# A graph-attention edge loop: q expanded by three bf16 products, item tables from DRAM

## The chip, the cores and the metric

One core of a Trainium2 chip runs the kernel, with its engines TensorE (PE), VectorE (DVE), ScalarE (ACT), GpSimd (POOL) and SyncE (SP), which work side by side and meet at semaphores. The metric is the device time of one execution in microseconds (us); lower is better. The time of a kernel is the median of its runs.

## The reference

Two layers on 6,250 nodes of 256 numbers, with 106,250 edges that are sorted by their destination node `dst`. First an attention over the edges, with 8 heads of 32, then a small mixture of 8 experts. What the change touches is the first:

```python
xn = layernorm(x)
q, k, v = xn @ Wq + bq, xn @ Wk + bk, xn @ Wv + bv       # per node, split in 8 heads of 32
e = edge_attr @ We                                       # per edge
alpha = sum(q[dst] * (k[src] + e), per head) / sqrt(32)  # per edge and head
alpha = softmax of alpha over the edges of one dst
out[dst] += (v[src] + e) * alpha                         # per node
x = x + out + xn @ Ws + bs
x = x + top-2-of-8 experts of layernorm(x)
```

## The kernel before

**Stages.** The program runs in stages, each a block with its own semaphores, one after the other. (1) The edge lists are cut into work items. (2) The projection: for each of 49 tiles of 128 nodes, q stays in SBUF as float32 (`q_sb`), k and v go to DRAM as `vk_table`, and the skip term goes to `skip_table`. (3) The edge loop. (4) Gates, layernorm and routing. (5) The experts, 105 blocks. (6) The output. The buffers of small tables in the later stages lie over those of the first: `src_idx`, `dst_loc`, `mask` and `q_sb` are used again under other names.

**Items.** An item is 128 edges and one tile of 128 nodes. A tile of 128 edges that spans two node tiles makes two items. There are 880 items in 55 chunks of 16. The loop is unrolled in the program over chunks (`c`) and items (`i`), and `par` is the chunk's parity.

**What an item does, in the order of its data:**
- SP loads 128 rows of `edge_attr` (`a_ring`, four deep, L727). POOL gathers 128 rows of v and k from `vk_table` by the indices `idx_c` (`kv_ring`, four deep, L743).
- PE turns `a_ring` by two transposes (L875), and ACT copies them to SBUF (`aT`, L827).
- PE multiplies `aT` by `We` into the left half of `ps_e` (two float32 products, L887). It then expands q: the one-hot `selT` (node by edge) times the node tile's q gives each edge the q of its destination, in the right half of `ps_e` (one float32 product of 256 columns, L890, with a column offset `n` in a register). The one-hot is made by ACT for four items at a time (`SEL = 4`), as relu(1 - |row - loc|), by L790 and L799, from `loc_c`, which SP loads for a whole chunk (bf16 numbers, broadcast to all partitions, L698).
- DVE adds e to v and k (`ve_ke`, L967), multiplies k by q (`kqq`, L973), and one item later reduces by head into `alpha` (L956).
- A chunk later, when the softmax of the chunk is known: POOL weighs v by the exponentials (`w_ring`, L753), ACT makes the one-hot of the other direction (`sel`, L805 and L809), PE sums by node (`ps_u`, L936), and DVE adds into `acc` (L1033).

**The softmax of a chunk** is spread over items of the next one by the tables `parts` of each engine. PE makes keys at item 0, scores at 3, minima at 6 and `turn_scores` at 10. DVE scans forward at 3 and back at 4, does `own` at 6, `least` at 7 and `shift` at 8. ACT makes `apart` at 3, `offs` at 4 and the exponentials at 11. POOL applies the mask at 5. DVE does these after the kqq of the same item, and the add to `acc` comes last.

**What sets the order.** Every engine runs its own list in order. PE's list for item i is: turn item i + 1, project item i (L887, L890), a softmax part if there is one, the sum of an item 13 behind. Its project of item i waits for ACT's `aT` of i and for DVE's `ve_added` and `kq_ready` of item i - 2, since `ps_e` has two buffers. The gather of item i waits for `ve_added` of item i - 4. These waits can be read in:

```python
pe.wait_ge(s["aT_ready"], at("aT_ready", c * CH + i))
pe.wait_ge(s["ve_added"], at("ve_added", c * CH + (i - 2)))
pe.wait_ge(s["kq_ready"], at("kq_ready", c * CH + (i - 2)))
```

PE runs a float32 product as two passes, so L887 shows four records an item and L890 two; a transpose shows one. In the projection, PE makes four products of 512 columns a tile (eight passes, L527), ACT copies the turned tile (L503), DVE adds the biases and stores k and v, skip and q (L561 to L565), and SP stores to DRAM.

Of the kernel before, what the change touches and what calls it, by code (L numbers as in the profile page):

```python
# [12 lines left out]
P = 128  # L13
# [16 lines left out]
def gnn_ffn(nc, x, src, dst, edge_attr, Wq, bq, Wk, bk, Wv, bv, We, Ws, bs, Wg, bg, gbias, W1, b1, W2, b2, out):  # L30
# [22 lines left out]
    with ExitStack() as ctx:  # L53
# [56 lines left out]
        loc_table = dram("loc_table", (NCH, CH * P), BF16)  # L110
# [9 lines left out]
        src_idx = sb("src_idx", [P, IT], I32)  # L120
        dst_loc = sb("dst_loc", [P, IT])
        mask = sb("mask", [P, IT])
        item_node_tile = sb("item_node_tile", [1, IT], I32)
        item_row = sb("item_row", [1, IT], I32)
        chunk_tile = sb("chunk_tile", [P, NCH])

        assert NT * NE <= IT and TOP * NT <= IT and NB <= IT
        assert 2 * NB <= IT
        take_i = src_idx[:, 0:NB]
        put_i = src_idx[:, NB:2 * NB]  # L130
        gate_w = dst_loc[:, 0:TOP * NT].rearrange("p (k j) -> p k j", k=TOP)
        logits = mask[:, 0:NT * NE].rearrange("p (j e) -> p j e", e=NE)
        block_expert = item_row[0:1, 0:NB]
        q_sb = sb("q_sb", [P, NT + 1, D])
# [12 lines left out]
        b4 = sb("b4", [P, 4 * D], F32, c_w4)  # L147
        tail_zeroed = sem("tail_zeroed", c_w4)
# [8 lines left out]
        with ExitStack() as c1:  # L157
# [29 lines left out]
            src_g = sb1("src_g", [P, IB, P], I32)  # L187
            sel_g = sb1("sel_g", [P, IB, P], I32)
            run_g = sb1("run_g", [P, IB, P], I32)
# [3 lines left out]
            m_lo = sb1("m_lo", [P, IT])  # L193
            m_hi = sb1("m_hi", [P, IT])
            run_h = flat(q_sb[:, :, :])[:, 0:IB * H * P].rearrange("p (b h e) -> p b h e", h=H, e=P)
            rest = flat(q_sb[:, :, :])[:, IB * H * P:]
# [47 lines left out]
            def _(sp):  # L244
# [16 lines left out]
                with nc.allow_non_contiguous_dma(reason="the short tail row of the edge lists"):  # L261
# [50 lines left out]
            def _(dve):  # L312
# [55 lines left out]
                v.tensor_copy(item_node_tile[:, :], node_tile_rep[0:1, :])  # L368
# [3 lines left out]
                v.tensor_copy(item_row[:, :], r_rep[0:1, :])  # L372
# [13 lines left out]
                for b in range(IB):  # L386
                    n = rows_in(b)
                    dve.wait_ge(turned, b + 1)
                    v.tensor_copy(src_idx[:, b * P:b * P + n], ps_src[:, 0:n])
                    v.tensor_copy(first_run[:, b * P // CH:(b * P + n) // CH], ps_src[:, P:P + n:CH])  # L390
                    v.tensor_copy(last_run[:, b * P // CH:(b * P + n) // CH], ps_src[:, 2 * P + CH - 1:2 * P + n:CH])
                    v.scalar_tensor_tensor(out=dst_loc[:, b * P:b * P + n], in0=node_tile_rep[:, b * P:b * P + n],
                                           scalar=-float(P), in1=ps_sel[:, 0:n], op0=ALU.mult,
# [4 lines left out]
                v.tensor_scalar(m_lo[:, :], dst_loc[:, :], 0.0, BIG, ALU.is_lt, ALU.mult)  # L398
                then(v.tensor_scalar(m_hi[:, :], dst_loc[:, :], P - 0.5, BIG, ALU.is_gt, ALU.mult))
                then(v.tensor_tensor(mask[:, :], m_lo[:, :], m_hi[:, :], ALU.add))  # L400
# [46 lines left out]
        with ExitStack() as c2:  # L447
# [3 lines left out]
            def ps2(name, shape):  # L451
# [14 lines left out]
            skip_out = [sb2(f"skip_out{i}", [P, D]) for i in range(2)]  # L466
            ps_t = [ps2(f"ps_t{i}", [P, 512]) for i in range(2)]
            ps_p = [ps2(f"ps_p{i}", [P, 1024]) for i in range(2)]
            s, at, grant = counters(c2, stat_ready=0, aggregated=0, ln_step=0, var_ready=0, sd_ready=0, xn_ready=0, xn_turned=2,
                                    xnT_ready=2, projected=2, q_out=2, kv_out_ready=2, skip_half=2, skip_out_ready=0,  # L470
# [12 lines left out]
            def _(sp):  # L483
# [8 lines left out]
                sp.wait_ge(stored[1], 16 + 32 * (NT // 2))  # L492

            @block.scalar
            def _(act):
# [1187 lines left out]
```

## Time and profile before

| | |
|---|---|
| median of 3 runs | 2812.76 us (2811.62 to 2814.19) |
| profiled execution | 2812.57 us, its span 2810.8 us |
| PE busy | 2503.2 us, 89% of the span |
| DVE busy | 2038.0 us, 73% |
| POOL busy | 1720.7 us, 61% |
| ACT busy | 1542.6 us, 55% |
| HBM | 173 GB/s over the span |
| mean granted PE clock | 0.952 of full |

Busy time is the time in which an engine executes. Registers, branches, semaphores and the issue of DMAs are not counted. The ends of matmuls are modelled, so records of PE overlap, and it is the distance between starts that tells the pace. An engine's idle time costs something only when that engine, or one that waits for it, is the bottleneck.

### The profile page before, as it was taken

Reading aid. Unit: us, or ns where it says so; the run is one execution under the profiler, and the core shown is the slowest. Engines: PE = TensorE matmul, PEld = TensorE weight load, DVE = VectorE, ACT = ScalarE, POOL = GpSimd, SP = SyncE. Lnnn points to the kernel's source line nnn. Section 1 sums busy time; section 2 is a strip of 40 time slices with the busy share of each in tenths; the row PEclk is TensorE's granted clock in tenths of the full one; section 3 lists DMA queues with packets and bytes.
Section 4 is the critical chain, followed back from the end, with each engine's and each line's share of the span. In section 5 each row is a group of like instructions: output and inputs, shape, how many; then the busy total and the mean of one; then the engine's idle time right before and its main releaser. Section 6 shows DMA issues by size and latency. Waiting matters only on the chain. (4 is left out here: it accounts for less than half of the span.)

```text
span 2810.8 us, 66316 instructions
## 1 busy us (share of the span) xinstructions
PE 2503.2 (89%) x13236; PEld 2104.1 (75%) x13237; DVE 2038.0 (73%) x5145; ACT 1542.6 (55%) x4238; POOL 1720.7 (61%) x2078
## 2 busy tenths in 40 slices
PE   1599699999999999999999999999994848999980
PEld 0244488888888888888888888888882837999980
DVE  2655689899999999999999999998996781111116
ACT  1011266666666666666666666666663224666650
POOL 3000278778788888888888888878886013555540
PEclk9999899999999999999999999999997568999995
DMA  6032577777777777777777777777771612222218
GB/s 215 33 109 107 161 226 212 210 212 215 216 215 213 212 213 212 217 214 218 215 208 216 211 214 221 214 211 209 213 206 58 206 58 66 71 71 69 71 60 274
DMA packets 304072, 490.05 MB, mean 174 GB/s; under 512 B 52058, under 2 KB 217692, under 8 KB 303580
## 3 DMA queue, kind: packets, MB, share of 16 engines
q0 software_dynamic: 81152, 259.63, 32.7%
q1 hardware_dynamic: 215548, 214.12, 23.6%
q10 hardware_dynamic: 7056, 12.85, 1.5%
q8 instruction: 105, 1.72, 0.3%
q14 instruction: 211, 1.73, 0.2%
HBM read 435.86 MB, written 51.41 MB: 173 GB/s over the span
## 5 line engine op out<-in xcount | busy, mean ns | idle before, releaser
L743 POOL DMA_INDIRECT kv_ring<-vk_table,idx_c x880 | 873.6, 993 | 601.3 <-DMA idx_c<-src_idx 238.6
L887 PE MATMUL ps_e<-we_sb,aT 128*128 128x256 f32 x3520 | 910.8, 381 | 12.5 <-DVE kqq L973 11.1
L967 DVE TENSOR_TENSOR ve_ke<-kv_ring,ps_e 128x512 f32<-128x512 f32 x880 | 601.8, 684 | 137.2 <-PE ps_e L890 116.8
L887 PEld LDWEIGHTS ps_e<-we_sb,aT 128*128 128x128 f32 x3520 | 602.2, 191 | 62.1 <-issue 12.7
L753 POOL TENSOR_TENSOR w_ring<-ve_ke,ea 128x264 f32<-128x264 f32 x880 | 558.8, 638 | 22.6 <-PE ps_u L936 6.2
L827 ACT COPY aT<-ps_t 128x256 f32<-128x256 f32 x880 | 326.5, 371 | 433.1 <-PE ps_t L875 422.4
L936 PE MATMUL ps_u<-w_ring,sel 128*128 128x264 f32 x1760 | 539.3, 388 | 8.1 <-DVE acc L1033 5.4
L890 PE MATMUL ps_e<-q_sb,selT 128*128 x1760 | 525.2, 380 | 0.0
L1033 DVE TENSOR_TENSOR acc<-acc,ps_u 128x264 f32 x880 | 369.2, 420 | 23.9 <-DVE acc L1021 12.1
L956 DVE TENSOR_REDUCE alpha<-kqq 128x8 f32<-128x256 f32 x880 | 366.4, 416 | 6.3 <-issue 4.2
L890 PEld LDWEIGHTS ps_e<-q_sb,selT 128*128 128x128 f32 x1760 | 335.6, 191 | 46.0
L973 DVE TENSOR_TENSOR kqq<-ve_ke,ps_e 128x256 f32<-128x256 f32 x880 | 361.2, 410 | 1.9
L936 PEld LDWEIGHTS ps_u<-w_ring,sel 128*128 128x128 f32 x1760 | 316.9, 191 | 57.5 <-POOL w_ring L753 16.4
L805 ACT ACTIVATE apart<-iota_free,dst_loc 128x128 f32<-128x128 f32 x880 | 348.8, 396 | 4.4 <-PE ps_u L936 4.1
L875 PE MATMUL ps_t<-ident,a_ring 128*128 128x128 f32 x1760 | 337.2, 274 | 13.4 <-DMA a_ring<-in_edge_attr 13.4
L875 PEld LDWEIGHTS ps_t<-ident,a_ring 128*128 128x128 f32 x1760 | 248.5, 142 | 115.2 <-DMA a_ring<-in_edge_attr 15.2
L809 ACT ACTIVATE sel<-apart 128x128 f32<-128x128 f32 x880 | 272.5, 310 | 105.6 <-ACT apart L805 2.8
L1611 DVE TENSOR_TENSOR y<-ps_y,acc 128x256 f32<-128x256 f32 x105 | 44.6, 425 | 361.2 <-PE ps_y L1580 361.2
L1494 POOL DMA_INDIRECT t_in<-xn_table,src_idx x105 | 102.5, 976 | 193.7 <-PE ps_t L1563 155.5
L1572 PE MATMUL ps_h<-tT,acc 128*128 128x128 f32 x1680 | 207.5, 277 | 1.8 <-ACT tT L1522 1.8
L1572 PEld LDWEIGHTS ps_h<-tT,acc 128*128 128x128 f32 x1680 | 198.6, 194 | 2.2 <-ACT tT L1522 2.2
L1580 PE MATMUL ps_y<-w_sb,hT 128*128 x840 | 198.6, 379 | 0.0
(248 smaller groups left out, 2538.1 us busy)
## 6 DMA issues: line engine op xcount, KB each, us to landing
a_ring<-in_edge_attr SPq DMA_DIRECT2D x880, 128.0 KB
loc_c<-loc_table SPq DMA_DIRECT2D x55, 512.0 KB, 5.9
kv_ring<-vk_table,idx_c POOLq DMA_INDIRECT x880
vk_table<-kv_out SPq DMA_DIRECT2D x49, 256.0 KB, 2.0
got<-y_table ACTq DMA_DIRECT2D x49, 256.0 KB, 3.8
skip_table<-skip_out SPq DMA_DIRECT2D x49, 128.0 KB, 1.7
skip<-skip_table SPq DMA_DIRECT2D x7, 896.0 KB, 7.2
xn_table<-acc SPq DMA_DIRECT2D x7, 896.0 KB, 4.9
```

Of the source, the lines that this page charges most:

```text
L743: g.indirect_dma_start(out=kv_ring[:, i % N_KV, :], out_offset=None, in_=vk_table, in_offset=bass.IndirectOffsetOnAxis(ap=idx_c[:, par, i: ...
L753: g.tensor_tensor(by_head(w_ring[:, i % N_W, :], CP), by_head(ve_ke[:, par * CH + i, :], CP), ea[par][:, i * H:(i + 1) * H][:, :, None].to ...
L805: nc.scalar.activation(apart[i % 2][:, :], iota_free[:, :], ACT.Abs, scale=-1.0, bias=dst_loc[:, bass.ds(m, 1)]).then_inc(s["apart_ready"], 1)
L875: last = t.transpose(ps_t[i % 2][:, k * P:(k + 1) * P], a_ring[:, i % N_A, k * P:(k + 1) * P], ident[:, :])
L887: t.matmul(ps_e[i % 2][:, 0:D], aT[i % 2][:, k * P:(k + 1) * P], we_sb[:, k, :], start=(k == 0), stop=(k == KD - 1))
L890: t.matmul(ps_e[i % 2][:, D:2 * D], selT[i // SEL % 2][:, i % SEL * P:(i % SEL + 1) * P], flat(q_sb[:, :, :])[:, bass.ds(n * D, D)], start ...
L936: t.matmul(ps_u[i % 2][:, 0:UW], sel[:, i % N_W, :], w_ring[:, i % N_W, :], start=True, stop=True).then_inc(s["summed"], 1)
L956: v.tensor_reduce(alpha[par][:, i * H:(i + 1) * H], by_head(kqq[i % 2][:, :], C), AX_X, ALU.add).then_inc(s["alpha_ready"], 1)
L967: v.tensor_tensor(both, kv.rearrange("p (t h c) -> p t h c", t=2, c=C), by_head(e, C)[:, None, :, :].to_broadcast([P, 2, H, C]), ALU.add). ...
L973: v.tensor_tensor(by_head(kqq[i % 2][:, :], C), by_head(ve_ke[:, ke, :], CP)[:, :, 0:C], by_head(ps_e[i % 2][:, D:2 * D], C), ALU.mult).th ...
L1033: v.tensor_tensor(a, a, ps_u[i % 2][:, 0:UW], ALU.add).then_inc(s["acc_added"], 1)
L1572: last = t.matmul(ps_h[par][:, f * P:(f + 1) * P], w1_now[par][:, k, f * P:(f + 1) * P], tT[par][:, k * P:(k + 1) * P], start=(k == 0), st ...
```

## The change

q is kept as three bf16 numbers whose sum is the float32 number exactly, and expanded by three bf16 products that are summed in PSUM; the one-hot is bf16 too. In the projection, ACT takes the first part, POOL what is left, ACT the second part, and POOL the third. The item tables (source index, destination in the tile, mask) lie in one buffer `tab` in the first stages, are stored once to DRAM, and SP loads 16 items of them per chunk into a ring of four. `loc` is loaded per four items into a ring of four, in place of a whole chunk. `kqq` is written in place over k + e; `least1`, `least2` and `shifted` become one buffer, as do some buffers of the first stage. Tables and buffers of the later stages lie in the room of q after `x1` (`spare_words`), with the same operations.

```diff
@@ tables
-        loc_table = dram("loc_table", (NCH, CH * P), BF16)
+        loc_table = dram("loc_table", (NCH * CH // SEL, SEL * P), BF16)
+        tab_table = dram("tab_table", (P, NCH * 3 * CH))
...
-        q_sb = sb("q_sb", [P, NT + 1, D])
+        q_parts = sb("q_parts", [P, 3, NT + 1, D], BF16)
...
+        tab = sb("tab", [P, NCH, 3, CH], F32, c_w4)
+        src_idx, dst_loc, mask = tab[:, :, 0, :].bitcast(I32), tab[:, :, 1, :], tab[:, :, 2, :]
@@ end of stage 1, SP and DVE
+                    sp.wait_ge(loc_ready, 2)
+                    sp.dma_start(tab_table, tab[:, :, :, :].rearrange("p n t i -> p (n t i)")).then_inc(tab_stored, 16)
...
+                dve.sem_inc(loc_ready, 1)
@@ projection: SP, ACT, POOL, DVE
+                sp.wait_ge(tab_stored, 16)
...
+                def first_part(j):
+                    act.wait_ge(s["q_out"], at("q_out", j))
+                    nc.scalar.copy(q_parts[:, 0, j, :], q_full[j % 2][:, :]).then_inc(s["q_part0"], 1)
+
+                def second_part(j):
+                    act.wait_ge(s["q_left_ready"], at("q_left_ready", j))
+                    nc.scalar.copy(q_parts[:, 1, j, :], q_left[j % 2][:, :]).then_inc(s["q_part1"], 1)
...
+                def first_left(j):
+                    pool.wait_ge(s["q_part0"], at("q_part0", j))
+                    if j >= 2:
+                        pool.wait_ge(s["q_part2"], at("q_part2", j - 2))
+                    g.tensor_tensor(q_left[j % 2][:, :], q_full[j % 2][:, :], q_parts[:, 0, j, :], ALU.subtract
+                                    ).then_inc(s["q_left_ready"], 1)
+
+                def third_part(j):
+                    pool.wait_ge(s["q_part1"], at("q_part1", j))
+                    g.tensor_tensor(q_parts[:, 2, j, :], q_left[j % 2][:, :], q_parts[:, 1, j, :], ALU.subtract
+                                    ).then_inc(s["q_part2"], 1)
...
-                    v.tensor_tensor(flat(q_sb[:, :, :])[:, bass.ds(j * D, D)], ps_p[par][:, 0:D], b4[:, 0:D], ALU.add).then_inc(s["q_out"], 1)
+                    dve.wait_ge(s["q_left_ready"], at("q_left_ready", j - 2))
+                    v.tensor_tensor(q_full[par][:, :], ps_p[par][:, 0:D], b4[:, 0:D], ALU.add).then_inc(s["q_out"], 1)
@@ edge loop, SP
-                        if i == 2 and more:
-                            sp.wait_ge(s["selT_ready"], at("selT_ready", c * (CH // SEL) - 1))
-                            load_loc(c + 1, 1 - par)
-                        if i == 8 and more:
-                            sp.wait_ge(s["ve_added"], at("ve_added", c * CH - 1))
-                            load_idx(c + 1, 1 - par)
+                        n = c * NLOC + i // SEL + NLOC - 1
+                        if i % SEL == 2 and n < NCH * NLOC:
+                            load_loc(n)
+                        if i == 8 and c + 1 < NCH:
+                            load_tab(c + 1)
...
+                def load_loc(n):
+                    if n >= NLOC:
+                        sp.wait_ge(s["apartT_ready"], at("apartT_ready", n - NLOC))
+                    sp.dma_start(loc_c[n % NLOC][:, :], loc_table[n:n + 1, :].to_broadcast([P, SEL * P])).then_inc(loc_loaded[n % NLOC], 16)
+
+                def load_tab(c):
+                    if c >= N_TAB:
+                        sp.wait_ge(s["ve_added"], at("ve_added", (c - N_TAB + 1) * CH - 1))
+                        sp.wait_ge(s["am_ready"], at("am_ready", c - N_TAB))
+                        sp.wait_ge(s["apart_ready"], at("apart_ready", (c - N_TAB + 1) * CH - 1))
+                    sp.dma_start(tab_c[:, c % N_TAB, :, :].rearrange("p t i -> p (t i)"),
+                                 tab_table[:, c * 3 * CH:(c + 1) * 3 * CH]).then_inc(tab_loaded[c % N_TAB], 16)
@@ edge loop, PE
-                    t.matmul(ps_e[i % 2][:, D:2 * D], selT[i // SEL % 2][:, i % SEL * P:(i % SEL + 1) * P], flat(q_sb[:, :, :])[:, bass.ds(n * D, D)],
-                             start=True, stop=True).then_inc(s["e_ready"], 1)
+                    for part in range(3):
+                        last = t.matmul(ps_e[i % 2][:, D:2 * D], selT[i // SEL % 2][:, i % SEL * P:(i % SEL + 1) * P],
+                                        q_parts[:, part, :, :].rearrange("p j d -> p (j d)")[:, bass.ds(n * D, D)],
+                                        start=(part == 0), stop=(part == 2))
+                    last.then_inc(s["e_ready"], 1)
@@ edge loop, DVE
+                    if c * CH + i >= 2:
+                        dve.wait_ge(s["alpha_ready"], at("alpha_ready", c * CH + i - 2))
...
-                    v.tensor_tensor(by_head(kqq[i % 2][:, :], C), by_head(ve_ke[:, ke, :], CP)[:, :, 0:C],
+                    v.tensor_tensor(by_head(ve_ke[:, ke, :], CP)[:, :, 0:C], by_head(ve_ke[:, ke, :], CP)[:, :, 0:C],
                                     by_head(ps_e[i % 2][:, D:2 * D], C), ALU.mult).then_inc(s["kq_ready"], 1)
```

## Rows read from the trace of the kernel before

**Rows 1.** The windows view, the edge loop over 52 chunks.
```profile
core 0: us, PE busy (x) PEld busy (x) DVE busy (x) ACT busy (x) POOL busy (x), PEclk, DMA share, GB/s
381.60:2088.39 1706.79, 1702.64 (x8945) 1466.29 (x8944) 1551.54 (x3849) 1142.64 (x3278) 1375.03 (x1718) 1.00 0.73 213
```

**Rows 2.** The timeline of PE (start, duration), first keys transpose of three chunks.
```profile
381.60 0.27 PE L911 MATMUL ps_ak<-ident,key_prev 128*128 128x128 f32 x1
...
1169.29 0.27 PE L911 MATMUL ps_ak<-ident,key_prev 128*128 128x128 f32 x1
...
2088.39 0.27 PE L911 MATMUL ps_ak<-ident,key_prev 128*128 128x128 f32 x1
```

**Rows 3.** The timeline of PE over the chunk that begins at 1201.94.
```profile
1201.94 0.27 PE L911 MATMUL ps_ak<-ident,key_prev 128*128 128x128 f32 x1
1202.05 0.27 PE L912 MATMUL ps_ak<-ident,run_c 128*128 128x128 f32 x1
...
1204.90 1.03 PE L887 MATMUL ps_e<-we_sb,aT 128*128 128x256 f32 x4
1205.77 0.59 PE L890 MATMUL ps_e<-q_sb,selT 128*128 x2
1206.20 0.61 PE L936 MATMUL ps_u<-w_ring,sel 128*128 128x264 f32 x2
...
1206.86 1.03 PE L887 MATMUL ps_e<-we_sb,aT 128*128 128x256 f32 x4
...
1217.97 0.59 PE L890 MATMUL ps_e<-q_sb,selT 128*128 x2
...
1221.03 1.03 PE L887 MATMUL ps_e<-we_sb,aT 128*128 128x256 f32 x4
...
1222.33 0.28 PE L927 MATMUL ps_rx<-ident,min_f 128*128 128x8 f32 x2
1222.46 0.37 PE L928 MATMUL ps_rx<-nident,min_l 128*128 128x8 f32 x2
```

**Rows 4.** The timeline of DVE in the same stretch; in brackets the idle time before.
```profile
1188.36 0.68 DVE L967 TENSOR_TENSOR ve_ke<-kv_ring,ps_e 128x512 f32<-128x512 f32 x1
...
1189.95 0.68 DVE L967 TENSOR_TENSOR ve_ke<-kv_ring,ps_e 128x512 f32<-128x512 f32 x1
...
1208.36 0.69 DVE L967 TENSOR_TENSOR ve_ke<-kv_ring,ps_e 128x512 f32<-128x512 f32 x1 [0.23 <-PE ps_e L890]
...
1219.26 0.69 DVE L967 TENSOR_TENSOR ve_ke<-kv_ring,ps_e 128x512 f32<-128x512 f32 x1
...
1220.25 0.41 DVE L973 TENSOR_TENSOR kqq<-ve_ke,ps_e 128x256 f32<-128x256 f32 x1
...
1225.78 0.69 DVE L967 TENSOR_TENSOR ve_ke<-kv_ring,ps_e 128x512 f32<-128x512 f32 x1 [1.40 <-DMA kv_ring<-vk_table,idx_c]
```

**Rows 5.** The timeline of POOL in the same stretch.
```profile
1221.15 0.98 POOL L743 DMA_INDIRECT kv_ring<-vk_table,idx_c  x1 [3.55 <-issue]
...
1230.20 0.99 POOL L743 DMA_INDIRECT kv_ring<-vk_table,idx_c  x1 [0.16 <-issue]
...
1232.01 0.99 POOL L743 DMA_INDIRECT kv_ring<-vk_table,idx_c  x1 [0.16 <-issue]
```

**Rows 6.** The page: groups (busy, mean ns, idle before) and DMA issues.
```profile
L753 POOL TENSOR_TENSOR w_ring<-ve_ke,ea 128x264 f32<-128x264 f32 x880 | 558.8, 638 | 22.6 <-PE ps_u L936 6.2
L827 ACT COPY aT<-ps_t 128x256 f32<-128x256 f32 x880 | 326.5, 371 | 433.1 <-PE ps_t L875 422.4
...
loc_c<-loc_table SPq DMA_DIRECT2D x55, 512.0 KB, 5.9
```

**Rows 7.** The timeline of the projection, PE's products of one tile.
```profile
153.02 3.60 PE L527 MATMUL ps_p<-w,xnT 128*128 128x512 f32 x8
```

**Rows 8.** The timeline where the projection ends and the loop begins.
```profile
296.30 0.42 DVE L563 TENSOR_TENSOR q_sb<-ps_p,b 128x256 f32<-128x256 f32 x1
...
297.07 0.34 SPq L488 DMA_DIRECT2D skip_table<-skip_out  x1
299.21 0.41 SPq L695 DMA_DIRECT2D we_sb<-in_L_gnn_We  x1
```

More of the change, by code:

```diff
@@ L1 @@
+import math
 from contextlib import ExitStack
@@ L466, in gnn_ffn @@
             skip_out = [sb2(f"skip_out{i}", [P, D]) for i in range(2)]
+            q_full = [sb2(f"q_full{i}", [P, D]) for i in range(2)]
+            q_left = [sb2(f"q_left{i}", [P, D]) for i in range(2)]
             ps_t = [ps2(f"ps_t{i}", [P, 512]) for i in range(2)]
@@ L598, in gnn_ffn @@
             aT = [sb3(f"aT{i}", [P, D]) for i in range(2)]
-            loc_c = [sb3(f"loc_c{i}", [P, CH * P], BF16) for i in range(2)]
-            apartT = sb3("apartT", [P, SEL * P])
-            selT = [sb3(f"selT{i}", [P, SEL * P]) for i in range(2)]
-            kqq = [sb3(f"kqq{i}", [P, D]) for i in range(2)]
+            NLOC = CH // SEL
+            loc_c = [sb3(f"loc_c{i}", [P, SEL * P], BF16) for i in range(NLOC)]
+            apartT = sb3("apartT", [P, SEL * P], BF16)
+            selT = [sb3(f"selT{i}", [P, SEL * P], BF16) for i in range(2)]
             ve_ke = sb3("ve_ke", [P, 2 * CH + 2, UW])
@@ L695, in _ @@
                 sp.dma_start(we_sb[:, :, :], We.rearrange("(k p) n -> p k n", p=P)).then_inc(s["const_loaded"], 16)
-                def load_loc(c, par):
-                    sp.dma_start(loc_c[par][:, :], loc_table[bass.ds(c, 1), :].to_broadcast([P, CH * P])).then_inc(loc_loaded[par], 16)
-                def load_idx(c, par):
-                    sp.dma_start(idx_c[:, par, :], src_idx[:, bass.ds(c * CH, CH)]).then_inc(idx_loaded[par], 16)
-                load_idx(0, 0)
-                load_loc(0, 0)
+                def load_loc(n):
[9 more added lines that the diff above has]
+                                 tab_table[:, c * 3 * CH:(c + 1) * 3 * CH]).then_inc(tab_loaded[c % N_TAB], 16)
+                load_tab(0)
+                for n in range(NLOC - 1):
+                    load_loc(n)
                 def load(c, par, steps):
-                    more = not (isinstance(c, int) and c == NCH - 1)
                     for kind, i, back in steps:
@@ L929, in emit @@
                             pe.wait_ge(s["shifted_ready"], at("shifted_ready", c - 1))
-                            t.transpose(ps_x, shifted[:, :], ident[:, :]).then_inc(s["shifted_turned"], 1)
+                            t.transpose(ps_x, least[:, :], ident[:, :]).then_inc(s["shifted_turned"], 1)
                         elif kind == "sum":
@@ L1079, in gnn_ffn @@
             NGR = len(groups)
-            skip = [sb4(f"skip{i}", [P, SG, D]) for i in range(2)]
+            skip = [spare_words(SG * D).rearrange("p (j d) -> p j d", d=D) for i in range(2)]
             xn2 = acc
```

148 lines of the change are left out of this document (91 added, 57 removed).

## The prediction

> **What bounds the kernel now.** I read the page's slices first, then the loop's window, then the timelines of TensorE (PE), VectorE (DVE) and GpSimd (POOL) over one chunk. The window of the loop, 52 chunks, shows PE busy 1702.6 of 1706.8 us at the full clock, DVE 1551.5 and POOL 1375.0 [rows 1]. A modelled busy share proves little, so the starts matter. From the first `keys` transpose of one chunk to the next is 32.65 us in an undisturbed chunk (1169.29 to 1201.94), and over 52 chunks the mean is (2088.39 - 381.60) / 52 = 32.82 us [rows 2, 3]. Inside a chunk, PE's starts leave no hole: an item without softmax work goes from 1204.90 to 1206.86, 1.96 us [rows 3], and items with such work are longer only by PE's own transposes. So 32.65 us is PE's own work, and 0.17 us a chunk is waiting. The edge loop is PE-bound, and it is 880 of such items.
>
> Second comes DVE: 1551.5 / 52 = 29.8 us busy a chunk [rows 1]; unhindered it takes 1.59 us for a plain item (1188.36 to 1189.95) [rows 4], the rest is the softmax. Third POOL: 1.81 us an item when it works without a pause (1230.20 to 1232.01) [rows 5], 29.0 us a chunk. Both lie below 32.65.
>
> **The q product.** It starts at 1205.77 and the sum product after it at 1206.20: 0.43 us for two passes of 256 float32 columns; the four passes ahead of it took 0.87, so 0.217 each [rows 3]. In place of two there are three bf16 products of 256 columns. No bf16 product is in the trace. From above, a product could last as long as a float32 pass, 0.217; from below, no record with its weight load comes closer than 0.065 (1222.33 to 1222.46 is two records of 8 columns) [rows 3]. Nearest is the single-pass transpose of 128 float32 columns, 0.11 us apart (1201.94 to 1202.05) [rows 3]: it streams 512 bytes a partition, just as 256 bf16 columns are 512 bytes, while a pass of 1 KB takes twice that. So 0.108 to 0.11 a product, 0.324 to 0.33 in place of 0.433: 0.105 less, times 880 is **92 us**. The ends: 3 x 0.065 would be 0.24 less an item, after which DVE's 29.8 a chunk would decide, and 3 x 0.217 would be 0.22 more.
>
> Each product carries its own load of the same one-hot. In the transposes a load goes with each product too and 0.11 holds for both [rows 3], so I take the loads as hidden.
>
> The trace agrees with the Trainium skill here (TensorE: Matmul & The Clock Gate, Back-to-back issue gap), which gives 256 / 2.4 + 2.5 = 109 ns between warm bf16 matmuls. The same page speaks against the change in LDWEIGHTS: 128 columns of weights take 128 / 1.2 = 107 ns, as long as the product itself; it also says that loads are pulled ahead of matmuls in flight. Were loads not hidden, by its figures the item would get 3 x (109 + 107) - 433 = 215 ns longer, some 3000 us in all (it is counted in rival D); hidden, the sum is the one above. Loads and products 0.065 apart in the trace speak against 107 ns of load standing between products.
>
> **What the shorter PE item uncovers.** PE would need 32.65 - 16 x 0.105 = 31.0 us a chunk; DVE's 29.8 and POOL's 29.0 stay below, but DVE's work is uneven. Items 3 to 8 hold scans, minima and shifts. DVE's item 3 starts at 1208.36 and item 8 at 1219.26, 10.90 us for five [rows 4]; PE ends the q product of item 3 at about 1205.77 + 1.96 + 0.59 = 1208.32 and of item 8 at 1217.97 + 0.59 = 1218.56 [rows 3], 10.24 us. DVE already falls 0.70 behind. PE's first product of item 10 (1221.03) needs the kqq of item 8 (ends 1220.25 + 0.41 = 1220.66) [rows 3, 4]: 0.37 us of margin. With five items 0.105 shorter DVE falls 0.53 further behind, and one more q product, 0.105, goes out of the margin: 0.37 - 0.53 - 0.105 = -0.27. So a new PE wait of about 0.25 us in each chunk, 55 x 0.25 = **14 us given back**. Bounds: 0, if DVE's present gaps take it up; at most, items 3 to 8 go at DVE's pace, 10.90 - (10.24 - 0.53) = 1.19 a chunk, 65 us.
>
> **POOL and the gathers.** POOL has some 3.55 us stalls (one ahead of the gather at 1221.15), after which DVE waits 1.40 us for kv rows at 1225.78 [rows 4, 5]. In such a chunk PE now loses up to 2 us; some eight in the loop, a shorter cover adds under 1 us each, within the 14. POOL's 29.0 against 31.0 leaves 2 us a chunk.
>
> **Queues.** `loc_table`'s 512 KB per chunk, 5.9 us to landing [rows 6], becomes four of 128 KB. SP issues three more DMAs a chunk, and one `tab` load takes the place of the index load. What is queued behind SP's new waits are the `a_ring` loads: `load_loc` waits for an `apartT` eight items or more old, `load_tab` for work of three chunks ago, so they pass at once. The loads are asked for seven items (13 us) or more before their reader; cost 0. If that cover were gone, 5.9 us a chunk would show. DMA engines are 0.73 busy [rows 1]; at 5% more pace 0.77. The smaller loc loads may even spare the kv rows a queue; I count nothing.
>
> **DVE, ACT, POOL in the loop.** kqq in place and `least` in one buffer move no element. DVE's new wait, on `alpha_ready` of two items before, is for an instruction of its own that ended before the last kqq began: 0. ACT and POOL do the same operations on other tiles; bf16 outputs count as unchanged, as ACT (1142.6 busy of 1706.8) is no bound [rows 1].
>
> **Projection.** The eight passes of a tile take PE 3.6 us [rows 7]. New per tile: two ACT copies (0.37 each, row L827) and two POOL subtractions of 256 elements (0.64, row L753 with 264) [rows 6]. ACT goes to 3 x 0.37, POOL to 1.3, DVE's wait for `q_left_ready` is two tiles old: hidden under 3.6. The last tile isn't: q ends at 296.30 + 0.42 = 296.72, then 0.37 + 0.64 + 0.37 + 0.64 and four hand-overs of about 0.1 end at 299.1; now the last store is issued at 297.07 and the next stage's first load at 299.21 [rows 8]. Cost 0 to 2, I take **1 us**. The `tab` store is issued while DVE makes its layernorm statistics and is waited for only after the projection: 0.
>
> **Sum.** The profiled execution took 2812.57 us (span 2810.8), the median is 2812.76, the same within 0.01%. 2812.8 - 92 + 14 + 1 = **2735 us**.
>
> **Rivals.**
> *A, the sum above*, waits from nothing to twice the estimate and a last-digit error of 0.003 on a product: 2720 to 2752. Chance 0.68.
> *B, DVE's burst decides*: all of items 3 to 8 go at DVE's pace, or POOL stalls make as much. 2812.8 - 92 + 65 = 2786 at most; range 2752 to 2786. For it: the margin of 0.37 is smaller than what is taken from it. Against: DVE's plain item of 1.59 against PE's 1.86 pays 0.27 back each time. Chance 0.15.
> *C, products closer than the transposes*: from 0.11 down to 0.065, DVE's and POOL's chunk of about 30 decides; 2812.8 - 2.8 x 55 = 2659 at the end. Against: one column a cycle fits all rows. Chance 0.04.
> *D, slower*: the three weight loads stand between the products. At the least spacing of a record with load, 0.065, each product takes 0.108 + 0.065 = 0.173, three 0.52 against 0.433: +0.086 x 880 = 76, 2889 us; streamed like float32 passes (0.217) it would be 0.65, +191. It decides from 0.036 us exposed per product on, (0.433 - 3 x 0.108) / 3. For it: three loads in place of two. Against: the transposes' 0.11. Chance 0.09.
> *E, no change*: a queue or code fetch eats it; the trace names none. Chance 0.04.
>
> **Numbers.** 2735; the range 2716 to 2780 holds A, most of B and the near edge of C, 0.83. Within 0.2% is what a measurement of this kernel can't tell from no change. Faster 0.87 (A, B, C), same 0.03, slower 0.10 (D and part of E).
>
> **What would show it.** L890 with three records an item, 0.11 apart; chunk to chunk 31.0 us in quiet chunks and 31.2 to 31.4 in most, with a wait for kqq at PE's L887 near item 10; DVE's busy share of the loop from 0.91 to about 0.95; loc landings well under 5.9 us; the projection at 3.6 a tile and the loop beginning within 2 us of now. I am wrong if L890's records stand more than 0.14 apart, if PE waits for DVE over 0.5 us in every chunk, or if kv rows become the wait that ends last.

## The result and the profile after

The changed kernel takes 2737.55 us (median of 4 runs, 2736.97 to 2739.12) against 2812.19 us for the kernel before in the same session (4 runs, 2811.59 to 2814.19): ratio 0.9734, 95% interval 0.9719 to 0.9749, faster by 2.7%. I had said 2735. The profiled execution took 2739.12 us, its span is 2737.3 us; it is 73.5 us shorter than that of before (2810.8), and that is the difference that the traces have to explain.

Line numbers move: L887 (We product) is L953 now, L890 (q) L957, L911 (first keys transpose) L980, L936 (sum) L1005, L956 (reduce) L1025, L967 and L973 (ve_ke, kqq) L1038 and L1044, L743 and L753 (gather, weigh) L805 and L815, L988 (the scan back) L1059.

The windows view over the same 52 chunks as [rows 1]:

```profile
core 0: us, PE busy (x) PEld busy (x) DVE busy (x) ACT busy (x) POOL busy (x), PEclk, DMA share, GB/s
381.12:2014.79 1633.67, 1626.53 (x9779) 1340.86 (x9777) 1531.79 (x3849) 1138.75 (x3278) 1382.73 (x1717) 1.00 0.78 224
```

1706.79 us became 1633.67, at the full granted clock as before. PE has 834 more matmul records (one more q product for each of 832 items, and two at the edges) and is 76 us less busy. DVE is 20 us less busy, which I had not expected; POOL is 8 us busier. Both come back at the experiments on DVE.

The timeline of PE over one nearly undisturbed chunk, and below it the page's two groups on the q product (busy us, mean ns of one, idle before):

```profile
1229.74 0.27 PE L980 MATMUL ps_ak<-ident,key_prev 128*128 128x128 f32 x1
...
1232.59 1.03 PE L953 MATMUL ps_e<-we_sb,aT 128*128 128x256 f32 x4
1233.46 0.49 PE L957 MATMUL ps_e<-q_parts,selT 128*128 x3
1233.79 0.61 PE L1005 MATMUL ps_u<-w_ring,sel 128*128 128x264 f32 x2
...
1234.45 1.03 PE L953 MATMUL ps_e<-we_sb,aT 128*128 128x256 f32 x4
...
1247.90 1.08 PE L953 MATMUL ps_e<-we_sb,aT 128*128 128x256 f32 x4
1248.82 0.49 PE L957 MATMUL ps_e<-q_parts,selT 128*128 x3
...
1260.86 0.27 PE L980 MATMUL ps_ak<-ident,key_prev 128*128 128x128 f32 x1
```
```profile
L957 PE MATMUL ps_e<-q_parts,selT 128*128 x2640 | 433.4, 273 | 0.0
L957 PEld LDWEIGHTS ps_e<-q_parts,selT 128*128 128x128 bf16 x2640 | 258.5, 98 | 137.6 <-issue 1.1
```

The reader is to see the distances of starts. The three bf16 products take 1233.79 - 1233.46 = 0.33 us, 0.109 each by the median over the loop, where the two float32 passes took 0.43 [rows 3]; the item takes 1234.45 - 1232.59 = 1.86 in place of 1.96 (medians 1.859 and 1.961). The busy figure of 273 ns a product is no pace: the next product starts 109 ns after it. A quiet chunk takes 31.07 or 31.08 us (23 of the 54 do; this one, with 31.12, is near) in place of 32.65. The mean over the 52 is (2014.79 - 381.12) / 52 = 31.42 in place of 32.82.

**Where the 73.45 us come from.** The 54 distances between first keys transposes, 351.32 to 2044.50, sum to 1693.18 us; before, 350.67 to 2119.31, to 1768.64. Had all shrunk like the quiet one, that would be 54 x 1.575 = 85.1 us. What the chunks are longer than a quiet one sums, over 52 of them, to 17.8 us now and 9.0 before; the first and the last chunk add 0.8: 9.6 us given back. The loop begins 0.65 us later, and what follows the last keys transpose takes 692.8 us in place of 691.5. -85.1 + 9.6 + 0.65 + 1.3 = -73.5. But the quiet chunk of now is not free of waits: 16 items that are each 0.102 shorter would make it 1.63 us shorter, not 1.575. The rows below show where the rest stays.

The timelines in the kernel after: DVE over the same chunk, then PE and DVE at items 8 to 10 of one of the longer chunks, and POOL at three of its stalls:

```profile
1235.85 0.69 DVE L1038 TENSOR_TENSOR ve_ke<-kv_ring,ps_e 128x512 f32<-128x512 f32 x1
...
1239.12 0.42 DVE L1059 TENSOR_TENSOR_SCAN scan_b<-resets,scan_f 128x128 f32<-128x128 f32 x1
...
1246.40 0.68 DVE L1038 TENSOR_TENSOR ve_ke<-kv_ring,ps_e 128x512 f32<-128x512 f32 x1
1247.00 0.41 DVE L1025 TENSOR_REDUCE alpha<-ve_ke 128x8 f32<-128x256 f32 x1
1247.33 0.41 DVE L1044 TENSOR_TENSOR ve_ke<-ve_ke,ps_e 128x256 f32<-128x256 f32 x1
```
```profile
1808.13 1.04 PE L953 MATMUL ps_e<-we_sb,aT 128*128 128x256 f32 x4
...
1810.32 1.10 PE L953 MATMUL ps_e<-we_sb,aT 128*128 128x256 f32 x4
1811.25 0.49 PE L957 MATMUL ps_e<-q_parts,selT 128*128 x3
...
1809.76 0.41 DVE L1044 TENSOR_TENSOR ve_ke<-ve_ke,ps_e 128x256 f32<-128x256 f32 x1
```
```profile
1184.76 0.99 POOL L805 DMA_INDIRECT kv_ring<-vk_table,tab_c  x1 [2.92 <-issue]
...
1399.82 0.99 POOL L805 DMA_INDIRECT kv_ring<-vk_table,tab_c  x1 [2.17 <-issue]
...
1829.80 0.95 POOL L805 DMA_INDIRECT kv_ring<-vk_table,tab_c  x1 [3.28 <-issue]
```

DVE's items 3 to 8 take 1246.40 - 1235.85 = 10.55 us, 0.35 less than before [rows 4]. The kqq of item 8 ends at 1247.33 + 0.41 = 1247.74, and PE's L953 of item 10 starts at 1247.90, one undisturbed item of 1.86 after that of item 9.

**The wait at item 10.** At first sight the wait that I had put there is missing. It is there, inside L953: from its start to that of L957 it takes 1248.82 - 1247.90 = 0.92 us, where the other items take 0.87 (1232.59 to 1233.46). The trace shows it pass by pass. In 52 of 53 chunks the second of the four passes of item 10 starts 0.437 to 0.440 us after the end of the kqq of item 8, however long the chunk is; in the kernel before, that holds in 7 chunks, and the median distance is 0.683. So DVE's kqq now holds PE up in nearly every chunk: by 0.06 us in the median, by 0.4 in the second example, where the item before takes 1810.32 - 1808.13 = 2.19 and L953 0.93. Over the 53 chunks the wait sums to 7.6 us (0.9 before).

### The profile page after: what moved, and what is told of

Read it like the earlier page. It is cut to its first block and busy times, and to the rows that moved or that the text cites. A ratio compares the mean times of both kernels' runs of the same rounds, so it can differ in the third digit from the quotient of the medians.

```text
span 2737.3 us, 70178 instructions
## 1 busy us (share of the span) xinstructions
PE 2420.9 (88%) x14116; PEld 1970.5 (72%) x14117; DVE 2024.7 (74%) x5145; ACT 1574.1 (58%) x4336; POOL 1792.4 (65%) x2176
## 3 DMA queue, kind: packets, MB, share of 16 engines
q8 instruction: 119, 1.95, 0.3%
## 5 line engine op out<-in xcount | busy, mean ns | idle before, releaser
L805 POOL DMA_INDIRECT kv_ring<-vk_table,tab_c x880 | 874.2, 993 | 283.5 <-issue 213.3
L953 PE MATMUL ps_e<-we_sb,aT 128*128 128x256 f32 x3520 | 914.5, 383 | 15.9 <-DVE ve_ke L1044 12.7
L1038 DVE TENSOR_TENSOR ve_ke<-kv_ring,ps_e 128x512 f32<-128x512 f32 x880 | 600.8, 683 | 80.1 <-PE ps_e L957 41.3
L953 PEld LDWEIGHTS ps_e<-we_sb,aT 128*128 128x128 f32 x3520 | 602.9, 191 | 69.3 <-issue 18.2
L815 POOL TENSOR_TENSOR w_ring<-ve_ke,ea 128x264 f32<-128x264 f32 x880 | 565.9, 646 | 22.9 <-PE ps_u L1005 6.8
L1005 PE MATMUL ps_u<-w_ring,sel 128*128 128x264 f32 x1760 | 542.1, 390 | 10.7 <-DVE acc L1104 5.5
L957 PE MATMUL ps_e<-q_parts,selT 128*128 x2640 | 433.4, 273 | 0.0
L1025 DVE TENSOR_REDUCE alpha<-ve_ke 128x8 f32<-128x256 f32 x880 | 365.3, 415 | 6.3 <-issue 3.9
L1044 DVE TENSOR_TENSOR ve_ke<-ve_ke,ps_e 128x256 f32<-128x256 f32 x880 | 360.9, 410 | 1.9
L957 PEld LDWEIGHTS ps_e<-q_parts,selT 128*128 128x128 bf16 x2640 | 258.5, 98 | 137.6 <-issue 1.1
L871 ACT ACTIVATE apart<-iota_free,tab_c 128x128 f32<-128x128 f32 x880 | 349.2, 397 | 4.3 <-PE ps_u L1005 3.9
L941 PE MATMUL ps_t<-ident,a_ring 128*128 128x128 f32 x1760 | 337.6, 274 | 13.2 <-DMA a_ring<-in_edge_attr 13.2
L941 PEld LDWEIGHTS ps_t<-ident,a_ring 128*128 128x128 f32 x1760 | 247.8, 142 | 112.5 <-DMA a_ring<-in_edge_attr 14.9
L1005 PEld LDWEIGHTS ps_u<-w_ring,sel 128*128 128x128 f32 x1760 | 267.8, 192 | 31.2 <-POOL w_ring L815 18.4
L1574 POOL DMA_INDIRECT q_parts<-xn_table,q_parts x105 | 101.7, 968 | 193.8 <-PE ps_t L1643 155.3
L1652 PE MATMUL ps_h<-q_parts,acc 128*128 128x128 f32 x1680 | 206.4, 276 | 3.6 <-ACT q_parts L1602 3.6
L1652 PEld LDWEIGHTS ps_h<-q_parts,acc 128*128 128x128 f32 x1680 | 197.5, 193 | 4.0 <-ACT q_parts L1602 4.0
L1660 PE MATMUL ps_y<-w_sb,q_parts 128*128 x840 | 198.7, 380 | 0.0
```

The lines of the kernel that those rows point to most:

```text
L805: g.indirect_dma_start(out=kv_ring[:, i % N_KV, :], out_offset=None, in_=vk_table, in_offset=bass.IndirectOffsetOnAxis(ap=tab_c[:, c % N_T ...
L815: g.tensor_tensor(by_head(w_ring[:, i % N_W, :], CP), by_head(ve_ke[:, par * CH + i, :], CP), ea[par][:, i * H:(i + 1) * H][:, :, None].to ...
L871: nc.scalar.activation(apart[i % 2][:, :], iota_free[:, :], ACT.Abs, scale=-1.0, bias=tab_c[:, c % N_TAB, 1, i:i + 1]).then_inc(s["apart_r ...
L941: last = t.transpose(ps_t[i % 2][:, k * P:(k + 1) * P], a_ring[:, i % N_A, k * P:(k + 1) * P], ident[:, :])
L953: t.matmul(ps_e[i % 2][:, 0:D], aT[i % 2][:, k * P:(k + 1) * P], we_sb[:, k, :], start=(k == 0), stop=(k == KD - 1))
L957: last = t.matmul(ps_e[i % 2][:, D:2 * D], selT[i // SEL % 2][:, i % SEL * P:(i % SEL + 1) * P], q_parts[:, part, :, :].rearrange("p j d - ...
```

## The experiments

All times beside their own runs of the kernel before. A quiet chunk is the distance of first keys transposes that comes most often (in x10, where none stands out, the shortest that repeats).

| run | what differs from the changed kernel | us | ratio to before, 95% interval | quiet chunk |
|---|---|---|---|---|
| x1 | q float32, one product | 2813.09 | 0.9998, 0.9988 to 1.0008 | 32.65 |
| x2 | x1, `loc` loaded by whole chunks | 2815.69 | 1.0007, 0.9997 to 1.0017 | 32.65 |
| x3 | two of the three products | 2710.65 | 0.9637, 0.9617 to 0.9657 | 30.28 |
| x4 | the third product twice | 2818.97 | 1.0023, 1.0014 to 1.0033 | 32.77 |
| x5 | six products of 128 columns | 2790.37 | 0.9928, 0.9911 to 0.9944 | 31.99 |
| x6 | DVE: one more reduce after kqq of item 7 | 2769.24 | 0.9855, 0.9838 to 0.9871 | 31.71 |
| x7 | the same after item 11 | 2738.52 | 0.9746, 0.9730 to 0.9762 | 31.07 |
| x8 | x3 with `kv_ring` eight deep | 2707.93 | 0.9640, 0.9624 to 0.9656 | 30.93 |
| x9 | `kv_ring` five deep | 2719.76 | 0.9673, 0.9657 to 0.9690 | 31.08 |
| x10 | one of the three products | 2686.68 | 0.9556, 0.9536 to 0.9575 | 29.6 |
| x11 | x6 with narrow weighing | 2754.39 | 0.9797, 0.9781 to 0.9813 | 31.40 |
| x12 | x3 with narrow weighing | 2676.84 | 0.9528, 0.9512 to 0.9544 | 29.71 |

### x1 and x2: is it the products or the loads?

```diff
-                    for part in range(3):
-                        last = t.matmul(ps_e[i % 2][:, D:2 * D], selT[...], q_parts[part ...],
-                                        start=(part == 0), stop=(part == 2))
+                    last = t.matmul(ps_e[i % 2][:, D:2 * D], selT[...], q_words[:, bass.ds(n * D, D)],
+                                    start=True, stop=True)
@@ x2 besides
-                        if i % SEL == 2 and n < NCH * NLOC:
-                            load_loc(n)
+                        if i == 2 and c + 1 < NCH:
+                            load_loc(c + 1)
```

> The changed kernel with its q expansion undone: q stays float32, one product of 256 float32 columns (two passes) with a float32 one-hot, no splitting in the projection. The DRAM tables, the loc loads per four items and the buffers written in place are kept. Theory P (the gain is PE's time in the q product): PE's quiet chunk is 32.65 us again, and the time is that of the kernel before less a few us for kv rows that come sooner: 2805 to 2813. Rival L (the gain comes from the smaller, smoother loads): under 2780, with a chunk below 32.4 us.

> As x1_f32q, and the loc rows are again loaded for a whole chunk of 16 items by one DMA of 512 KB. Theory P: 2810 to 2816, at most 5 us above x1_f32q, since the kernel before lost 16.5 us of DVE time, but little of PE's, to kv rows that came late. Rival L: 20 us or more above x1_f32q.

Measured 2813.09 and 2815.69, each with an interval that holds 1. With everything else of the change in place and q as float32, the time is that of before: the tables in DRAM, the small `loc` loads, kqq in place and the shared buffers are worth nothing and cost nothing that can be measured. The whole gain comes from the products.

### x3, x4 and x10: what one product is worth

```diff
-                    for part in range(3):
+                    PARTS = (0, 1)            # x4: (0, 1, 2, 2)    x10: (0,)
+                    for k, part in enumerate(PARTS):
```

> The changed kernel with two of the three bf16 products; the third part of q is left out of the expansion (the splitting stays). Theory P with an uneven DVE as the next bound: PE's own chunk becomes 31.07 - 16 x 0.111 = 29.3 us, below DVE's 29.8 us of work, so the chunk stays at 30.1 to 30.5 and the time is 2665 to 2695, with PE waiting for DVE in most chunks. Rival (nothing but PE's products matters): all of 0.111 x 880 = 98 us is gained, 2640.

> The changed kernel with four bf16 products; the third part of q is added twice. Theory P: PE is the bound at three products, so a fourth costs all of its 0.111 x 880 = 98 us less the waits that it covers (up to 10): 2826 to 2836, about 15 to 20 above the kernel before. Rival (DVE or POOL is the bound of the changed kernel already): under 2800.

> The changed kernel with the first of the three bf16 products alone: q is expanded by its bf16 part only, the two smaller parts are left out of the sum. Theory: TensorE's item is 1.64 us, but VectorE's softmax burst and GpSimd decide, as they already did with two products (2710.7 us, where 2640 was TensorE's own): almost nothing more is gained, 2690 to 2710. Rival: TensorE still decides and the third product is worth what the others are, 2612 to 2640.

A fourth product costs 2818.97 - 2737.55 = 81 us, 7 us under the range that I gave, a miss; its item takes 1.97 us, 0.109 more, 96 us over 880 items. The other 15 are waits that it covers: item 10 is held by kqq in 5 chunks in place of 52, and what the chunks are longer than a quiet one falls from 17.8 to 8.1 us. Taking the third away gives back only 27 us in place of 98, a miss. The item falls to 1.75 us as expected, but the quiet chunk to 30.28 where PE's own work would be 31.07 - 16 x 0.11 = 29.3: PE waits ahead of items 4, 10 and 0 (item 3 to 4 takes 2.18 in place of 1.86, 9 to 10 takes 2.10 and 15 to 0 takes 1.95 in place of 1.75). My expectations for x11 and x12 name these places one item too low, as 2, 8 and 14 and as "item 8 to 9". The second product away brings 24 us more, a little beyond the range that I gave. So the three-product kernel stands at the edge: one product more counts for 81 of 96 us, one less for 27 of 98.

### x5: do the weight loads cost?

```diff
-                    for part in range(3):
-                        last = t.matmul(ps_e[i % 2][:, D:2 * D], ...)
+                    for h in range(2):
+                        for part in range(3):
+                            last = t.matmul(ps_e[i % 2][:, D + h * P:D + (h + 1) * P], ..., start=(part == 0), stop=(part == 2))
```

> The changed kernel with each q product cut in two of 128 columns: six products, each with its own weight load, for the same columns. It measures what a weight load costs when the stream is too short to cover it. Theory P (a load with its product can't come closer than the 0.065 us seen for records of 8 columns): six at 0.065 make 0.39 in place of 0.333, +0.057 x 880 = 50 us, 2780 to 2795. If loads cost nothing at all, 2738 to 2745. Rival D (a load of 128 columns takes 107 ns of its own): 6 x 0.107 = 0.64, +270 us, above 2950.

The same columns with twice the loads. The timeline of PE in x5 (its L958 is the q product, L1006 the sum, L941 the transposes):

```profile
1210.52 0.50 PE L958 MATMUL ps_e<-q_parts,selT 128*128 x6
1210.85 0.66 PE L1006 MATMUL ps_u<-w_ring,sel 128*128 128x264 f32 x2
1211.35 0.38 PE L941 MATMUL ps_t<-ident,a_ring 128*128 128x128 f32 x2
```

Six products start within 1210.85 - 1210.52 = 0.33 us, 0.056 apart by the median, so even here no load stands between products. The price falls behind them: the sum's two passes take 0.50 us to the next start in place of 0.44 or 0.45, and the item 1.92. Whether it is the six loads or the six shorter products that delay the sum, this run can't tell, since it doubles both. 0.06 x 880 = 53 us is what was measured (2790.37 - 2737.55). The time lies in the range of my theory, but not for its reason: records do come closer than 0.065. That bound was a mean of two distances, 0.03 and 0.11. A reader who looks at the doubled operation alone would find it free.

### x6, x7 and x11: DVE's burst

```diff
+                            if i == 7:        # x7: i == 11
+                                v.tensor_reduce(idle_out[:, 0:H], idle_in, AX_X, ALU.add)
@@ x11 besides, in weigh
+                    width = CP if isinstance(c, int) and c == 0 else 1
-                    g.tensor_tensor(by_head(w_ring[...]), by_head(ve_ke[...]), ...
+                    g.tensor_tensor(by_head(w_ring[...])[:, :, 0:width], by_head(ve_ke[...])[:, :, 0:width], ...
```

> The changed kernel with one extra DVE operation a chunk, a reduction of 128x256 numbers into a buffer that nobody reads, after the kqq of item 7, inside DVE's burst. Theory P (DVE's lag in items 3 to 8 is within 0.1 to 0.2 us of holding PE up): 0.33 us more lag gives 0.15 to 0.33 us of PE wait a chunk, +8 to +18 us, 2746 to 2756. Rival (DVE has 1.5 us a chunk to spare wherever it falls): 2738 to 2741.

> The same extra DVE operation after the kqq of item 11, outside the burst, where DVE has caught up. Theory P: hidden, 2737 to 2742. If DVE's total load were what counts, the same as x6_dve7.

> The kernel of x6 (the changed kernel with an extra 128x256 reduce on VectorE after the kqq of item 7), in which GpSimd weighs from the second chunk on only the first of 33 columns of each head, 8 columns in place of 264; the rest of the weighted row keeps what the first chunk left there, so this part of the sum is left out. Theory (VectorE's minima run long in x6 because GpSimd's weighing runs at the same time): the second least operation falls from a mean of 0.65 us back to about 0.35, the distance from item 8 to 9 on TensorE from 2.48 to about 2.19 (1.86 plus the 0.33 of the extra operation), a quiet chunk from 31.71 to about 31.4, and the time from 2769 to between 2740 and 2755 us. Rival (the long minima come from something else, the PSUM or TensorE's reads): least stays at 0.65, 2.48 stays, and only what GpSimd's spare time covers of its own stalls is gained: 2758 to 2769 us.

The same 0.33 us of DVE costs 32 us at item 7 and 1 us at item 11: it is the burst of items 3 to 8 that reaches PE, at item 10. But x6 cost more than expected, 2769 against at most 2756: PE's distance from item 9 to 10 is 2.48, 0.62 above 1.86, for an operation of 0.33. The groups of DVE in the window 400 to 2000 show the rest; first the kernel before, then after, x6 and x11:

```profile
L988 DVE TENSOR_TENSOR_SCAN scan_b<-resets,scan_f 128x128 f32<-128x128 f32 x48 | 33.0, 687 | 0.0
L1005 DVE SCALAR_TENSOR_TENSOR least<-off_last,min_l,least 128x128 f32<-128x128 f32 x48 | 17.2, 358 | 1.7
```
```profile
L1059 DVE TENSOR_TENSOR_SCAN scan_b<-resets,scan_f 128x128 f32<-128x128 f32 x51 | 22.3, 438 | 0.0
L1077 DVE SCALAR_TENSOR_TENSOR least<-off_last,min_l,least 128x128 f32<-128x128 f32 x51 | 18.2, 358 | 1.8
```
```profile
L1083 DVE SCALAR_TENSOR_TENSOR least<-off_last,min_l,least 128x128 f32<-128x128 f32 x51 | 33.4, 654 | 1.8
```
```profile
L1085 DVE SCALAR_TENSOR_TENSOR least<-off_last,min_l,least 128x128 f32<-128x128 f32 x51 | 18.3, 358 | 1.8
```

The same operation of the same size takes 0.36 or 0.65 us. In x11, where POOL's weighing (0.64 us) is cut to 0.22, it is back at 0.358, the distance from item 9 to 10 falls to 2.17, the quiet chunk from 31.71 to 31.40, and the time by 15 us (0.31 x 54 = 17), all as the theory had it. That POOL's wide weighing lengthens these operations is thereby shown. And 31.40 is 0.33 above the 31.07 of the changed kernel, the whole of the added operation: DVE has no slack left in the burst.

A rival would be POOL's gather, which runs beside the long operation too. The timelines of x6 and of x11 settle it:

```profile
1231.71 0.99 POOL L811 DMA_INDIRECT kv_ring<-vk_table,tab_c  x1 [0.25 <-issue]
1232.18 0.66 DVE L1083 SCALAR_TENSOR_TENSOR least<-off_last,min_l,least 128x128 f32<-128x128 f32 x1
1232.72 0.64 POOL L821 TENSOR_TENSOR w_ring<-ve_ke,ea 128x264 f32<-128x264 f32 x1
```
```profile
1225.60 0.99 POOL L812 DMA_INDIRECT kv_ring<-vk_table,tab_c  x1 [1.39 <-DVE ve_ke L1046]
1226.07 0.35 DVE L1085 SCALAR_TENSOR_TENSOR least<-off_last,min_l,least 128x128 f32<-128x128 f32 x1
1226.62 0.22 POOL L823 TENSOR_TENSOR w_ring<-ve_ke,ea 128x8 f32<-128x8 f32 x1
```

In both, `least` starts 0.47 us into the gather. Only the weighing behind it differs. How they share is plainest in `scan_b`; the timeline of POOL and DVE in the kernel before, then POOL's in the one after:

```profile
1211.48 0.64 POOL L753 TENSOR_TENSOR w_ring<-ve_ke,ea 128x264 f32<-128x264 f32 x1
...
1211.74 0.67 DVE L988 TENSOR_TENSOR_SCAN scan_b<-resets,scan_f 128x128 f32<-128x128 f32 x1
```
```profile
1239.16 0.79 POOL L815 TENSOR_TENSOR w_ring<-ve_ke,ea 128x264 f32<-128x264 f32 x1
```

Before, the scan starts 0.26 us into the weighing and takes 0.67. After, it starts (1239.12, shown above) 0.04 before the weighing; it takes 0.42 and the weighing 0.79 in place of 0.64. Here whoever comes second pays. Over the 52 chunks that is 13 of the 20 us by which DVE is less busy (52 scans of 438 ns in place of 687), and most of the 8 by which POOL is busier (the one weighing a chunk that takes 0.79 in place of 0.64). The Trainium skill (SBUF — State Buffer, Who interferes with whom) describes such a lock: a DVE operation with two inputs in SBUF and a GpSimd operation that reads SBUF exclude each other for a whole instruction; the trace agrees that the second waits, though the scan that waited ended 0.29 us after the weighing, 0.13 less than its own 0.42. All 47 long scans of the kernel before end 0.29 after a weighing. The long `least` of x6 does not fit this order: it begins 0.54 us ahead of the weighing's record and ends 0.12 into it. POOL's records are rough, and that detail stays open.

### x8, x12 and x9: POOL's stalls, and what bounds next

```diff
@@ x8, with x3's two products
-N_KV = 4
+N_KV = 8
@@ x9, all three products
-N_KV = 4
+N_KV = 5
-            loc_c = [sb3(f"loc_c{i}", [P, SEL * P], BF16) for i in range(NLOC)]
+            N_LOC = 2
+            loc_c = [sb3(f"loc_c{i}", [P, SEL * P], BF16) for i in range(N_LOC)]
-            LAG = dict(weigh=FIRST_WEIGH + N_KV,
+            LAG = dict(weigh=FIRST_WEIGH + 4,
```

> As x3_two (two products, the third part of q left out), with a ring of eight kv buffers in the room of the unused part of q, in place of four; the index of weigh in POOL's list is unchanged, and some semaphores are shared to make room for the new ones. Theory S (most of the waiting over the quiet chunk comes from POOL's 2 to 3.5 us stall once in 110 gathers, which the gathers could run ahead of): of the 0.565 us a chunk over the quiet 30.28 half goes, 2690 to 2702. Rival (POOL can't run further ahead because its weigh operations wait for the sums, or the stall hits the mask and not the gathers): within 4 us of x3_two's 2710.7.

> The kernel of x3 (two of the three bf16 products, the third part left out) with the same narrow weighing, 8 columns in place of 264 from the second chunk on. Theory (with two products it is VectorE, lengthened by GpSimd's weighing, and GpSimd itself that take the gain, in waits at items 2, 8 and 14): a quiet chunk falls from 30.28 to TensorE's own, 31.07 - 16 x 0.11 = 29.3 to 29.6, and the time from 2710.7 to between 2648 and 2675 us. Rival (VectorE's own amount of work decides, whatever GpSimd does): a quiet chunk of 29.9 or more, 2690 us or more.

> The changed kernel with kv_ring five deep in place of four; to make room the ring of loc tiles is two deep in place of four, the sum and weigh lags stay in the order that the deeper ring gives them. Nothing is left out. Theory (GpSimd's stalls of 2 to 4 us, one in 110 gathers, make up most of what the changed kernel lost beyond my estimate, about 15 of the 18 us by which its 55 chunks are longer than a quiet one): one more item of cover, 1.9 us, takes away about half of each stall's cost, 2726 to 2733 us. Rival 1: a ring of five brings new collisions between VectorE's minima and GpSimd's weighing in every chunk, as eight slots did: 2738 to 2750, with quiet chunks above 31.2. Rival 2: the stalls reach TensorE by GpSimd's mask or weighing and not by the kv rows, so that the ring is no help: 2736 to 2739, with the same seven long chunks.

*x8.* The long chunks of x3, 32 to 35 us, are gone, and most chunks take about 30.93. So are POOL's stalls themselves: x3 has seven of 1.7 to 3.6 us, 110 gathers apart, in the loop, and x8 one, of 2.71 us ahead of the gather at 1148.84. Why, no run shows. It is no faster: with POOL earlier, the minima meet its weighing, the first takes 0.69 and the second 0.61 us on average, and item 9 to 10 takes 2.93. Theory S missed; the rival's number held, though not for its reason.

*x12.* With narrow weighing x3 gives 34 of its 71 missing us back; the quiet chunk is 29.71, against 29.3 of PE's own. 2676.84 lies 2 us outside the theory's range and far from the rival's 2690. Half of what two products lost was POOL's weighing, in DVE's operations and in POOL's own time (the waits ahead of items 4 and 0 are gone); most of the rest is DVE's burst (item 9 to 10 still takes 2.15, 0.40 x 54 = 22 of 37 us).

*x9* is the fastest complete kernel, 2719.76. The quiet chunk is unchanged at 31.08. The long ones are shorter: the stall chunks and those after them are 6.1 us above quiet in place of 14.1, the others 2.4 in place of 3.7. PE's wait at item 10 is not: it sums to 10.3 us in place of 7.6. POOL's stalls themselves are as long as ever, now 109 gathers apart:

```profile
1381.38 0.96 POOL L806 DMA_INDIRECT kv_ring<-vk_table,tab_c  x1 [3.47 <-issue]
```

It lies 6 us below the theory's range, because the loop's edges are shorter too: the loop begins 1.7 us earlier, the first chunk takes 28.15 us in place of 29.80, and what follows the last keys transpose 686.3 in place of 692.8 (x8 also has 686.9 there; the changed kernel and its eight variants with a ring of four have 690.0 to 692.8). That this is the deeper ring is argued from these numbers; x9 also halves the ring of `loc` and shifts the weighing. Theory right in kind, both rivals dead.

## Why the prediction came out right, by its steps

**The q product: 92 us foreseen, 90 measured.** The mechanism held: the products stand 0.109 us apart like the transposes, which move the same 512 bytes a partition. The item is 0.102 shorter and not 0.105, since the sum behind the products gives back 0.002; 0.102 x 880 = 90 us. x1 shows that nothing else of the change has a part in it, and x4, x3 and x10 price the fourth, third and second product at 0.109 us of PE's item each.

**DVE's burst: 14 us foreseen, with POOL's stalls counted in; 12.7 measured for both.** Between the first and the last keys transpose lie 864 items, 864 x 0.102 = 88.1 us; the distances shrank by 75.4, so 12.7 were given back. PE's wait for kqq at item 10 is 6.7 of them (7.6 against 0.9), 4.8 in chunks that no stall touches. The mechanism is the one forecast, a PE wait for kqq at item 10 in nearly every chunk, but the usual size is 0.06 us where I had worked out 0.27, and longer waits in 18 chunks make up the rest of the sum. Two errors in that working stood against each other. I took DVE's 10.90 us for items 3 to 8 as a fixed amount of work; it held a `scan_b` of 0.67 us that was long only because POOL's weighing ran beside it. At the new pace the scan starts 0.04 us ahead of the weighing, takes 0.42, and the burst 10.55; 0.25 of the 0.35 is the scan, and 0.11 is item 3, 1.96 in place of 2.07, where DVE waits for PE's q product both times. And I took the hand-over from DVE to PE as nothing: the second pass of L953 starts 0.44 us after the end of kqq and 0.22 after the first, so kqq must end 0.22 ahead of the first, and the margin of 0.37 was one of 0.15. -0.27 + 0.35 - 0.22 = -0.14; the last 0.08, down to 0.06, are smaller differences, such as 1.34 in place of 1.40 us from DVE's item 8 to the end of its kqq. That the collision went away was luck of phase: x6 brings one back and pays twice for 0.33 us, x11 pays once, and nothing of it is hidden.

**POOL's stalls: under 1 us each, "some eight".** They come once in 110 gathers (1184.76 to 1399.82 is 215.1 us, 110 items at 1.96), seven times in the loop. The stall chunks and those after them rose from 8.0 to 14.1 us above quiet; without their waits at item 10 the rise is 5.1 us, 0.7 per stall. The last 0.9 of the 12.7 is in the first and the last chunk. The size was right.

**The rest.** Loads, queues, kqq in place at nothing: right (x1, x2). The trace of after gives no landing time for the `loc` loads, so that "well under 5.9" is neither shown nor refuted. The projection keeps its pace, 3.60 us of products a tile, and the loop begins 0.65 us later (1 foreseen), with 1.3 us after the loop that I had not counted.

```profile
154.15 3.60 PE L583 MATMUL ps_p<-w,xnT 128*128 128x512 f32 x8
```

My sum was -92 + 14 + 1 = -77; the traces say -88.1 + 12.7 + 2 = -73.5 (the other 16 items lie outside these distances). The largest error of a term is 4 us. Of what I had said would show the theory right, the quiet chunk (31.07), the spacing of 0.11, the wait near item 10 and the begin of the loop came true; that most chunks take 31.2 to 31.4 did not, and DVE's share is 0.94, not 0.95.

**The rivals.** *B*, all of items 3 to 8 at DVE's pace, is dead at three products (2752 to 2786); but DVE does decide item 10, with no slack left (x6, x11). *C*, closer products, is dead: 0.109.
## What to carry to other kernels

Read pace from distances of starts, and price a replaced product by the nearest product that moves the same bytes a partition. Before a duration of a crowded stretch is taken as work, look for the same operation elsewhere in the trace: if it also appears at two thirds of the time, the difference is a collision and will move with the pace. Before a wait is called missing, look inside the instruction group that it should stand in front of: here the wait sits between the first and the second pass. When an engine with rare long stalls feeds the bottleneck through a ring, one more slot can be worth a fifth of the whole change's gain and more (x9: 18 us for 2 KB a partition), but it shifts the phase between engines, and x8 shows that this can take everything back.

## What the runs showed of the hardware

- POOL stands still for 2 to 4 us before one gather in every 110 (each 128 rows of 2 KB) with a ring of four: 225.5 us apart before, 215.7 after. With a ring of five (x9) it is one in 109, and with eight (x8) there is one such stall in the whole loop. The trace names no releaser; the cause is open.
- DVE operations with two SBUF inputs (scan, scalar_tensor_tensor of 128x128) take 0.34 to 0.42 us alone and up to 0.90 (x8) beside POOL's 128x264 product; POOL's product takes 0.64 alone and 0.79 when it starts 0.04 us after the scan.
- PE's second pass behind a semaphore wait starts 0.44 us after the end of the DVE instruction that it waited for, in 52 of 53 chunks; an undisturbed second pass starts 0.22 after the first.
- bf16 products of 256 columns with a load each start 0.109 us apart. With 128 columns they start 0.056 apart, six in a row, and delay the float32 product behind them by 0.05 to 0.06.
